# Two chained depthwise convolutions on TensorE: operand produced in two pieces, a shorter normalisation, the middle product kept in the output tile

## The chip, the cores and the metric

The kernel runs on one core of one Trainium2 chip. The metric is device time of one execution in microseconds (us). TensorE (PE) multiplies matrices and has a separate weight-load path (PEld), VectorE (DVE) and ScalarE (ACT) work elementwise, GpSimd (POOL) makes differences of columns, and SyncE (SP) issues nearly all DMAs.

## The reference

Everything is fp32. `x` is (32, 192, 56, 56). Twice, `x` is group-normalised (32 groups of 6 channels) and convolved channel by channel, and the result is added to `x`: first with a 31x31 filter and a bias, then with an 11x11 filter that is built from four points.

```python
def _gn(v, G=32, eps=1e-05):
    B_, C_, H_, W_ = v.shape
    g = v.reshape(B_, G, C_ // G, H_, W_)
    m = jnp.mean(g, axis=(2, 3, 4), keepdims=True)
    s = jnp.var(g, axis=(2, 3, 4), keepdims=True)
    return ((g - m) / jnp.sqrt(s + eps)).reshape(v.shape)

x = x + _L0_conv_ref(_gn(x), L0_conv_weight, L0_conv_bias_term)
x = x + _L1_conv_ref(_gn(x), L1_conv_weight_coord, L1_conv_radius, L1_conv_weights)
```

## The kernel before, in words

**Tiling.** The 128 partitions hold 4 bands of 16 image rows times 32 images. A job is one channel of one convolution, so there are 384 jobs: 192 FIRST jobs (31x31) and 192 SECOND jobs (11x11). They alternate in the list `PATTERN`: 12 slots, slots 0, 2, ..., 10 FIRST and 1, 3, ..., 11 SECOND. One turn of the loop over groups runs the 12 slots; iterations 0, 1 and the last ones are written out, 2 to 30 are a loop on DVE and ACT (2 to 29 on SP, 2 to 31 on PE and POOL). The second convolution of a group lags its first by some slots, since it needs the first one's sums for its own normalisation.

**One job on the engines.** ACT normalises a channel of `raw` into `images` (`normalise`, L763). DVE transposes it by 32x32 blocks into `xt` (`transpose_in`, L985). POOL makes differences of even and odd columns (`differences`: for FIRST L736, 960 columns, then L737, 512 columns, the differences of halves; for SECOND L739, 960 columns). ACT rounds the operand to its high part `x_hi` (`high`, L774 and L776) and DVE subtracts to get the low part `x_lo` (`low`, L1004 and L1006). PE then multiplies by banded (Toeplitz) matrices `toep` that DMAs fill from DRAM (L535), in three matmuls for each matrix: hi by hi, hi by lo, lo by hi (L1226). A FIRST job has 36 matmuls of 192 or 224 columns on the last 768 columns of its operand (the inner products: one of halves, two that share bank 3), then 48 of 352 to 448 columns on the first 960 columns (the outer products). A SECOND job has 9 inner matmuls (the middle product, bank 0) and 18 outer ones. At the end, ACT copies the middle product from PSUM to `p2` (`copy_p2`, L785 for FIRST, L788 for SECOND), DVE adds it to the halves (`combine`, L1013, FIRST alone) and to the outer products (`outputs`, L1023), transposes back into `yt` (`transpose_out`, L1032) and adds that to `raw` (`add_residual`, L1041).

**The order.** Each engine's order is written out by hand; semaphores tie them. While PE works on job n+1, DVE finishes job n and prepares job n+2 (`AHEAD` = 2). PE starts a job when `lo_ready` says that all of its `x_lo` is there, and when the outputs of the job two before have left PSUM. `T_RING` = 2: a channel's matrices are loaded over those of the channel two before, after that job's `conv_done`. SP goes through the same 12 slots: for each job it waits for `conv_done`, issues 8 DMAs of matrices, at slot 7 the four loads of a later group's `x`, at slots 5 and 11 the four stores of three channels.

**The normalisation.** `statistics` (L976) leaves 6 numbers for each half band of a channel (7 half bands, 6 channels). `normalisation` turns these into scale and bias in a chain of small DVE instructions, each waiting for the one before through `norm_chain` (`settle`). Two slots of a loop turn have it: slot 2 (for the second convolution of the group before) and slot 8 (for the first convolution of the next group). There it is split: `normalisation_begins` (aggregations L920 and L921, copies L926) stands ahead of `transpose_in`, `normalisation_ends` (L935 to L965) behind it, ahead of `combine`. ACT takes the root between (L792).

## Time and profile before

| | us |
|---|---|
| median of 3 runs (3794.69 to 3796.62) | 3796.46 |
| the profiled execution's own time | 3793.75 |
| its span | 3792.0 |
| PE busy | 3529.6 (93%) |
| DVE busy | 3284.3 (87%) |
| ACT busy, POOL busy | 1203.3, 1130.2 |
| granted TensorE clock, mean | 0.969 of full speed |
| DMA | 587.51 MB, mean 155 GB/s |

A busy share is time in which the engine had an instruction running. A window of the profile gives the same shares for a stretch, with the granted clock (1.00 is full speed) and the mean busy share of the 16 DMA engines, which goes to about 1.2 where they are full.

### The profile page before, as it was taken

What the parts mean: (1) busy time and instruction counts of PE and PEld (TensorE: products, weight loads), DVE (VectorE), ACT (ScalarE), POOL (GpSimd) and SP (SyncE); (2) the same over time, 40 slices, a digit from 0 to 9 for tenths busy, and PEclk for the clock granted to TensorE, in tenths of its full rate; (3) what the DMA queues carried; (4) which work ended last, traced back from release to release, by engine and by line L of the source; (5) the groups of instructions that cost most, each with busy time, mean ns of one, the idle gap of its engine ahead of it and who ended that gap; (6) DMA issues with size and microseconds to landing.
All of it is one profiled execution on the core that took longest, in us unless ns stands there. A gap on an engine that the chain in (4) does not pass through costs nothing.

```text
span 3792.0 us, 65954 instructions
## 1 busy us (share of the span) xinstructions
PE 3529.6 (93%) x21312; PEld 3349.7 (88%) x21312; DVE 3284.3 (87%) x4851; ACT 1203.3 (32%) x1442; POOL 1130.2 (30%) x660
## 2 busy tenths in 40 slices
PE   5889999999999999999999999999999999999997
PEld 5889898898898898988988988989889889899896
DVE  7888898888988888988889888889888898888887
ACT  3333333333333333333333333333333333333332
POOL 6113332223332233332223323333223323233332
PEclk9999999999999999999999999999999999999999
DMA  9987887879877878878788778888787887788673
GB/s 183 199 174 152 156 159 148 155 156 170 155 145 148 167 153 156 161 147 155 158 165 156 145 147 165 156 156 158 149 156 157 163 158 145 147 166 168 121 141 82
DMA packets 896128, 587.51 MB, mean 155 GB/s; under 512 B 501656, under 2 KB 858136, under 8 KB 895576
## 3 DMA queue, kind: packets, MB, share of 16 engines
q1 hardware_dynamic: 895416, 585.62, 80.2%
q14 instruction: 152, 1.25, 0.1%
q10 hardware_dynamic: 544, 0.38, 0.1%
q8 instruction: 16, 0.26, 0.0%
HBM read 499.20 MB, written 86.61 MB: 154 GB/s over the span
## 4 chain that ended last, share of the span: by engine, by line
PE 51%; DVE 28%; issue 15%; SPq 2%; POOL 1%; DMA 1%; DVEq 1%; ACT 0%; POOLq 0%; ACTq 0%
PE acc L1226 51%; DVE acc L1023 5%; DVE yt L1032 5%; DVE x_lo L1006 4%; DVE halves_tmp L939 3%; SPq L535 2%; DVE halves_tmp L941 2%; DVE part L976 1%; DVE raw L1041 1%; DVE p L1013 1%; DVE norm L965 1%; DMA toep<-padded 1%; DVE halves L926 1%; DVE x_lo L1004 0%; DVE agg L921 0%
## 5 line engine op out<-in xcount | busy, mean ns | idle before, releaser
L1226 PE MATMUL acc<-x_hi,toep 128*112 128x224 f32 (+5 forms) x14208 | 3406.6, 330 | 255.3 <-DVE x_lo L1006 178.0
L1226 PEld LDWEIGHTS acc<-x_hi,toep 128*112 128x112 f32 x14208 | 2454.5, 188 | 383.9 <-issue 182.3
L1226 PE MATMUL acc<-x_lo,toep 128*112 128x224 f32 (+5 forms) x7104 | 2343.7, 330 | 0.0
L1226 PEld LDWEIGHTS acc<-x_lo,toep 128*112 128x112 f32 x7104 | 1333.5, 188 | 51.0
L739 POOL TENSOR_TENSOR xt<-xt 128x960 f32<-128x960 f32 x188 | 423.6, 2253 | 1535.1 <-DVE xt L985 1535.1
L776 ACT ACTIVATE x_hi<-xt 128x256 fp32r<-128x256 f32 (+1 forms) x384 | 347.5, 905 | 1212.7 <-POOL xt L739 1193.9
L1023 DVE TENSOR_TENSOR acc<-acc,p 128x896 f32<-128x896 f32 x384 | 418.6, 1090 | 342.2 <-PE acc L1226 340.1
L736 POOL TENSOR_TENSOR xt<-xt 128x960 f32<-128x960 f32 x180 | 406.9, 2261 | 1016.8 <-DVE xt L985 1016.8
L774 ACT ACTIVATE x_hi<-xt 128x1472 fp32r<-128x1472 f32 x192 | 275.5, 1435 | 770.4 <-POOL xt L737 682.1
L985 DVE STREAM_TRANSPOSE xt<-images 128x960 f32<-128x960 f32 x384 | 451.1, 1175 | 14.0 <-ACT images L763 1.3
L1041 DVE TENSOR_TENSOR raw<-yt,raw 128x896 f32 (+1 forms) x384 | 422.4, 1100 | 30.3 <-DVE yt L1032 12.9
L763 ACT ACTIVATE images<-raw,norm 128x896 f32 (+1 forms) x384 | 439.3, 1144 | 16.8 <-DVE norm L965 16.8
L976 DVE BATCH_NORM_STATS2 part<-raw 96x6 f32 (+3 forms) x768 | 443.0, 609 | 0.0
L1032 DVE STREAM_TRANSPOSE yt<-acc 128x896 f32<-128x896 f32 x384 | 424.6, 1106 | 9.5
L1006 DVE TENSOR_TENSOR x_lo<-xt,x_hi 128x256 fp32r<-128x256 f32 (+1 forms) x384 | 396.7, 1033 | 3.1 <-ACT x_hi L776 3.1
L1004 DVE TENSOR_TENSOR x_lo<-xt,x_hi 128x1472 fp32r<-128x1472 f32 x192 | 317.3, 1653 | 3.6 <-ACT x_hi L776 3.6
L737 POOL TENSOR_TENSOR xt<-xt 128x512 f32<-128x512 f32 x180 | 231.8, 1288 | 0.0
L792 ACT ACTIVATE small<-small 32x1 f32<-32x1 f32 x64 | 12.9, 202 | 469.6 <-DVE small L947 469.6
L1013 DVE TENSOR_TENSOR p<-acc,p 128x448 f32<-128x448 f32 x192 | 116.8, 608 | 36.4 <-ACT p L785 29.1
L788 ACT ACTIVATE p<-acc 128x448 f32<-128x448 f32 x192 | 102.7, 535 | 100.6 <-DVE acc L1023 62.5
L939 DVE TENSOR_SCALAR halves_tmp<-halves,small 32x7 f32<-32x7 f32 x64 | 125.9, 1968 | 2.2
L785 ACT ACTIVATE p<-acc,bias_all 128x224 f32<-128x224 f32 x192 | 81.4, 424 | 0.0
(62 smaller groups left out, 456.2 us busy)
## 6 DMA issues: line engine op xcount, KB each, us to landing
toep<-padded SPq DMA_DIRECT2D x384, 322.0 KB
toep<-padded SPq DMA_DIRECT2D x384, 273.0 KB
toep<-padded SPq DMA_DIRECT2D x384, 217.0 KB
out_dram<-raw SPq DMA_DIRECT2D x189, 336.0 KB, 5.6
raw<-in_x_dram SPq DMA_DIRECT2D x93, 672.0 KB, 11.7
toep<-padded SPq DMA_DIRECT2D x768, 58.5 KB
toep<-padded SPq DMA_DIRECT2D x384, 80.5 KB
toep<-padded SPq DMA_DIRECT2D x384, 47.2 KB
```

The costliest lines, as they stand in the source:

```text
L736: nc.gpsimd.tensor_tensor(differences_held(), shifted_even(), repeated_odd(), ALU.subtract)
L739: nc.gpsimd.tensor_tensor(differences_held(), repeated_odd(), shifted_even(), ALU.subtract).then_inc(xd_ready, 1)
L763: nc.scalar.activation(image(ring(i, s, I_RING))[:, :, 1:1 + W], raw_rows(g, c), ACT.Identity, bias=norm[:, 0:1], scale=norm[:, 1:2]).then ...
L776: nc.scalar.activation(high_part, source, ACT.Copy).then_inc(hi_ready, 1)
L976: nc.vector.bn_stats(parts[0:held, k, c, :], raw_channel(g, c)[0:held, k * HALF:(k + 1) * HALF]).then_inc(parts_ready, 1)
L985: nc.vector.transpose(transposed(), blocks(image(ring(i, s, I_RING)))[:, :, ::-1, :]).then_inc(xt_ready, 1)
L1004: nc.vector.tensor_tensor(low_part, source, high_part.bitcast(F32), ALU.subtract)
L1006: nc.vector.tensor_tensor(low_part, source, high_part.bitcast(F32), ALU.subtract).then_inc(lo_ready, 1)
L1023: nc.vector.tensor_tensor(outer(i, s), outer(i, s), p2[:].unsqueeze(1).to_broadcast([P, 2, JH * B]), ALU.add).then_inc(y_ready, 1)
L1032: nc.vector.transpose(yt[:].rearrange("p (i s b) -> p s i b", s=2, b=B), outer(i, s).rearrange("p s (i b) -> p s i b", b=B)).then_inc(imag ...
L1041: nc.vector.tensor_tensor(rows, yt[:].rearrange("p (j h e) -> p h j e", h=HB, e=2), rows, ALU.add).then_inc(residual_added, 1)
L1226: last = nc.tensor.matmul(dst, toeplitz(toep, f, place_of_toep, part, w), src[:, cols], start=(m == matrices[0][0] and part == 0 and src i ...
```

## The change

**Operand in two pieces.** The 768 inner columns of a FIRST operand (480 of a SECOND one) are made, rounded and subtracted first, and the 960 outer ones after them, each with semaphores of its own. PE starts a job at `lo_inner_ready` and waits for `lo_ready` ahead of its outer products. On POOL and in the early iterations on DVE the differences of halves now come first, then a new copy of the 256 member columns to a contiguous place, then the 960-column difference.

**Normalisation in 15 steps.** The two aggregations, four copies and a hand-made mean and variance over 7 halves are replaced by four copies that gather all 6-number entries of an image (up to 72 columns of 32 partitions each) into `yt`, one `bn_aggr` over the 252 numbers, and one `tensor_scalar`; this stands whole ahead of `transpose_in`. The rest, from the reciprocal on, stands in slots 2 and 8 now behind `transpose_out` and the new `low_inner`.

**Middle product in the output tile.** `p2` is now `yt[:, 0:448]`, so ACT's copy of it waits for `residual_added` of the job before in place of `y_ready` of it.

```diff
-NORM_STEPS = 22
+NORM_STEPS = 15
@@ tiles
-        p2 = sb("p2", [P, JH * B])
         yt = sb("yt", [P, N])
+        p2 = yt[:, 0:JH * B]
+        gathered = yt[0:B, JH * B:JH * B + HALVES * CG * 6]
@@ operands
+        def inner_operand(i, s, tile):
+            if PATTERN[s][0] == FIRST:
+                start, size, at = AT_D2, N_HALVED * B, place(i, s) + 2 * N_D
+            else:
+                start, size, at = AT_EVEN + 1, N_D, place(i, s)
+            return xt[:, start * B:start * B + size], tile[:, at:at + size]
+        def outer_operand(i, s, tile):
+            at = place(i, s) + (0 if PATTERN[s][0] == FIRST else N_D)
+            return xt[:, AT_D * B:AT_D * B + 2 * N_D], tile[:, at:at + 2 * N_D]
@@ gpsimd, differences (FIRST)
-                    nc.gpsimd.tensor_tensor(differences_held(), shifted_even(), repeated_odd(), ALU.subtract)
-                    nc.gpsimd.tensor_tensor(*differences_of_halves(), ALU.subtract).then_inc(xd_ready, 1)
+                    nc.gpsimd.tensor_tensor(*differences_of_halves(), ALU.subtract)
+                    nc.gpsimd.tensor_copy(*members()).then_inc(xd_inner_ready, 1)
+                    nc.gpsimd.tensor_tensor(differences_held(), shifted_even(), repeated_odd(), ALU.subtract
+                                            ).then_inc(xd_ready, 1)
@@ scalar, high
-                act.wait_ge(xd_ready, n + 1)
+                if PATTERN[s][0] == FIRST:
+                    act.wait_ge(xd_inner_ready, first_ordinal(i, s) + 1)
+                else:
+                    act.wait_ge(xt_ready, n + 1)
...
+                source, high_part = inner_operand(i, s, x_hi)
+                nc.scalar.activation(high_part, source, ACT.Copy).then_inc(hi_inner_ready, 1)
+                act.wait_ge(xd_ready, n + 1)
+                source, high_part = outer_operand(i, s, x_hi)
                 nc.scalar.activation(high_part, source, ACT.Copy).then_inc(hi_ready, 1)
@@ scalar, copy_p2
-                    act.wait_ge(y_ready, n)
+                    act.wait_ge(residual_added, n)
@@ vector, normalisation_begins
-                link(nc.vector.bn_aggr(agg[:, 0, :], parts[:, 0].rearrange("p c k -> p (c k)")))
-                link(nc.vector.bn_aggr(agg[0:B * (BANDS - 1), 1, :],
-                                       parts[0:B * (BANDS - 1), 1].rearrange("p c k -> p (c k)")))
-                settle()
+                if positive(added):
+                    dve.wait_ge(residual_added, added)
                 for q in range(BANDS):
                     held = min(2, HALVES - 2 * q)
-                    link(nc.vector.tensor_copy(halves[:, :, 2 * q:2 * q + held].rearrange("b s k -> b k s"),
-                                               agg[B * q:B * q + B, 0:held, :]))
+                    link(nc.vector.tensor_copy(gathered[:, q * 2 * CG * 6:(q * 2 + held) * CG * 6],
+                                               parts[B * q:B * q + B, 0:held].rearrange("p k c n -> p (k c n)")))
...
+                link(nc.vector.bn_aggr(small[:, 2:4], gathered))
+                dve.wait_ge(norm_chain, f * NORM_STEPS + done[0])
+                nc.vector.tensor_scalar(small[:, 4:5], small[:, 3:4], EPS, None, ALU.add).then_inc(var_ready, 1)
@@ vector, normalisation_ends: the seven instructions ahead of the reciprocal
-                link(nc.vector.tensor_reduce(small[:, 0:1], halves[:, 0, :], AX_X, ALU.add))
...
-                link(nc.vector.tensor_scalar(halves_tmp[:, 0, :], halves[:, 0, :], small[:, 6:7], None, ALU.subtract))
-                settle()
-                link(nc.vector.tensor_tensor(halves_tmp[:, 1, :], halves_tmp[:, 0, :], halves_tmp[:, 0, :], ALU.mult))
...
@@ vector, the FIRST slots of the loop
-                        if early1:
-                            normalisation_ends(i * 2 + 1, norm1, job(i, LAST_FIRST) + 1)
                         combine(i, s)
...
                         outputs(i, s)
                         transpose_out(i, s)
+                        if after and not low_first:
+                            low_inner(*after)
+                        if early2:
+                            normalisation_ends(norm2_ordinal(group2), norm2, normalised)
+                        if early1:
+                            normalisation_ends(i * 2 + 1, norm1, job(i, LAST_FIRST) + 1)
                         if after and not low_first:
                             low(*after)
                         add_residual(i, s)
@@ tensor
-                    if k == before_outer and positive(n + 1 - P_RING):
-                        pe.wait_ge(image_ready, n + 1 - P_RING)
+                    if k == before_outer:
+                        pe.wait_ge(lo_ready, n + 1)
+                        if positive(n + 1 - P_RING):
+                            pe.wait_ge(image_ready, n + 1 - P_RING)
...
-                    pe.wait_ge(lo_ready, n + 1)
+                    pe.wait_ge(lo_inner_ready, n + 1)
```

On DVE at slot 8 of the loop, from the end of slot 7 to the transpose of the operand of slot 10 (L9xx are lines of each kernel; `parts1_ready` counts the statistics), before:

```order
L1006 TENSOR_TENSOR x_lo<-xt,x_hi 128x1440 [waits hi_ready]
L918 ISA
L919 MEMSET small 32x1 [waits parts1_ready]
L920 BN_AGGR agg<-part 128x2
L921 BN_AGGR agg<-part 96x2
L916 ISA
L926 COPY halves<-agg 32x2x2 [waits norm_chain]
L926 COPY halves<-agg 32x2x2 x2
L926 COPY halves<-agg 32x2
L982 REGISTER_ALU
L985 STREAM_TRANSPOSE xt<-images 128x15x2x32 [waits lo_ready,xn_ready]
```

The same place now:

```order
L1014 TENSOR_TENSOR x_lo<-xt,x_hi 128x960 [waits hi_ready]
L933 ISA
L934 MEMSET small 32x1 [waits parts1_ready]
L939 COPY yt<-part 32x72 [waits residual_added]
L939 COPY yt<-part 32x72 x2
L939 COPY yt<-part 32x36
L941 ISA
L942 MEMSET small 32x1 [waits norm_chain]
L943 BN_AGGR small<-yt 32x2
L944 REGISTER_ALU
L945 TENSOR_SCALAR small<-small 32x1 [waits norm_chain]
L986 REGISTER_ALU
```

The aggregation and the variance now both stand ahead of the transpose.

On DVE at the same slot, the stretch behind that transpose, from the last step of the normalisation to the residual, before:

```order
L965 COPY norm<-small 32x2 x3
L932 REGISTER_ALU
L1012 REGISTER_ALU [waits p2_copied,norm_chain]
L1013 TENSOR_TENSOR p<-acc,p 128x2x7x32 [waits u_done]
L1023 TENSOR_TENSOR acc<-acc,p 128x2x448 [waits conv_done,comb_ready]
L1032 STREAM_TRANSPOSE yt<-acc 128x2x14x32 [waits residual_added,y_ready]
L1004 TENSOR_TENSOR x_lo<-xt,x_hi 128x1472 [waits hi_ready]
L1006 TENSOR_TENSOR x_lo<-xt,x_hi 128x256
L1041 ISA [waits image_ready]
```

Now (the four steps between the reciprocal and the first copy left out):

```order
L989 STREAM_TRANSPOSE xt<-images 128x15x2x32 [waits lo_ready,xn_ready]
L1020 REGISTER_ALU [waits p2_copied]
L1021 TENSOR_TENSOR yt<-acc,yt 128x2x7x32 [waits u_done]
L1031 TENSOR_TENSOR acc<-acc,yt 128x2x448 [waits conv_done,comb_ready]
L1040 STREAM_TRANSPOSE yt<-acc 128x2x14x32 [waits residual_added,y_ready]
L1008 TENSOR_TENSOR x_lo<-xt,x_hi 128x768 [waits hi_inner_ready]
L952 REGISTER_ALU
L953 RECIPROCAL small<-small 32x1 [waits std_ready]
...
L969 COPY norm<-small 32x2 x3
L950 REGISTER_ALU
L1014 TENSOR_TENSOR x_lo<-xt,x_hi 128x960 [waits hi_ready,norm_chain]
L1049 ISA [waits image_ready]
```

The outputs, the transpose back and the inner `x_lo` now stand ahead of the reciprocal, where the whole rest of the normalisation stood ahead of them.

## Rows read from the trace of the kernel before

**Rows 1.** The page, busy time, share of the span and instructions of each engine.

```profile
PE 3529.6 (93%) x21312; PEld 3349.7 (88%) x21312; DVE 3284.3 (87%) x4851; ACT 1203.3 (32%) x1442; POOL 1130.2 (30%) x660
```

**Rows 2.** Waits of PE, whole span: line, what ended it, us, times, longest.

```profile
PE acc L1226 <- DVE x_lo L1006: 178.0, 61, 6.8
```

**Rows 3.** Timeline of DVE, four `outputs`: start us, us, instruction [idle before <-releaser].

```profile
1011.07 1.10 DVE L1023 TENSOR_TENSOR acc<-acc,p 128x896 f32<-128x896 f32 x1 [1.67 <-PE acc L1226]
...
1051.16 1.10 DVE L1023 TENSOR_TENSOR acc<-acc,p 128x896 f32<-128x896 f32 x1 [4.68 <-PE acc L1226]
...
1068.95 1.10 DVE L1023 TENSOR_TENSOR acc<-acc,p 128x896 f32<-128x896 f32 x1 [1.83 <-PE acc L1226]
...
1127.01 1.10 DVE L1023 TENSOR_TENSOR acc<-acc,p 128x896 f32<-128x896 f32 x1 [1.67 <-PE acc L1226]
```

**Rows 4.** Timeline of DVE at slot 8.

```profile
1023.13 0.32 DVE L920 BATCH_NORM_AGGREGATE agg<-part 128x2 f32<-128x36 f32 x1
...
1023.65 0.73 DVE L926 COPY halves<-agg 32x4 f32<-32x4 f32 x4
1024.42 1.18 DVE L985 STREAM_TRANSPOSE xt<-images 128x960 f32<-128x960 f32 x1
...
1025.84 2.12 DVE L939 TENSOR_SCALAR halves_tmp<-halves,small 32x7 f32<-32x7 f32 x1
1027.99 1.20 DVE L941 TENSOR_TENSOR halves_tmp<-halves_tmp 32x7 f32<-32x7 f32 x1
...
1030.01 0.15 DVE L949 RECIPROCAL small<-small 32x1 f32<-32x1 f32 x1 [0.27 <-ACT small L792]
...
1031.10 0.73 DVE L965 COPY norm<-small 32x2 f32<-32x2 f32 x4
...
1032.62 1.10 DVE L1023 TENSOR_TENSOR acc<-acc,p 128x896 f32<-128x896 f32 x1
```

**Rows 5.** Timeline of POOL in the same slot.

```profile
1025.68 2.26 POOL L736 TENSOR_TENSOR xt<-xt 128x960 f32<-128x960 f32 x1 [6.02 <-DVE xt L985]
1027.89 1.28 POOL L737 TENSOR_TENSOR xt<-xt 128x512 f32<-128x512 f32 x1
```

**Rows 6.** Line L939: count, duration ns min/median/max, first and last start.

```profile
L939 DVE TENSOR_SCALAR halves_tmp<-halves,small x64: 218/2114/2122, 26.4 to 3720.9; 32x7 f32<-32x7 f32 x64
```

**Rows 7.** Timeline of PE: slot 10's first matmul; slot 0's second matmul and its first outer `x_lo`.

```profile
1036.83 0.53 PE L1226 MATMUL acc<-x_hi,toep 128*112 128x224 f32 x1 [2.77 <-DVE x_lo L1006]
...
1056.31 0.27 PE L1226 MATMUL acc<-x_lo,toep 128*112 128x224 f32 x1
...
1060.18 0.36 PE L1226 MATMUL acc<-x_lo,toep 128*112 128x448 f32 x1
```

**Rows 8.** Window of PE: from, to, us, PE busy, granted clock, DMA share, GB/s.

```profile
1036.90:1040.00 3.10, 3.10 (x17) 0.50 1.22 204
```

**Rows 9.** Groups by form, 1000 to 3000 us: shapes, count | busy us, mean ns.

```profile
L1004 DVE TENSOR_TENSOR x_lo<-xt,x_hi 128x1472 fp32r<-128x1472 f32 x103 | 169.9, 1650 | 0.0
L774 ACT ACTIVATE x_hi<-xt 128x1472 fp32r<-128x1472 f32 x103 | 147.8, 1435 | 391.7 <-POOL xt L737 391.7
...
L1006 DVE TENSOR_TENSOR x_lo<-xt,x_hi 128x256 fp32r<-128x256 f32 x103 | 42.6, 414 | 0.0
...
L921 DVE BATCH_NORM_AGGREGATE agg<-part 96x2 f32<-96x36 f32 x35 | 8.9, 254 | 0.0
```

**Rows 10.** Timeline of the DMA issues on SP.

```profile
1041.08 6.32 SPq L535 DMA_DIRECT2D toep<-padded  x8
...
1051.25 6.13 SPq L535 DMA_DIRECT2D toep<-padded  x8
...
1069.60 6.25 SPq L535 DMA_DIRECT2D toep<-padded  x8
```

**Rows 11.** Windows: from, to, us, busy PE, PEld, DVE, ACT, POOL, clock, DMA share, GB/s.

```profile
1078.00:1087.00 9.00, 9.00 (x51) 8.60 (x50) 8.50 (x15) 2.44 (x3) 3.30 (x2) 1.00 1.18 211
...
1088.00:1089.00 1.00, 1.00 (x7) 0.90 (x5) 0.80 (x6) 1.00 (x1) 0.00 (x0) 1.00 0.69 100
```

More of the change, by code:

```diff
@@ L66 @@
 AT_D2 = AT_D + 2 * JE
-AT_ODD = AT_D2 + 2 * JZ + 1
+AT_MEMBERS = AT_D2 + 2 * JZ
+AT_ODD = AT_MEMBERS + JZ + 1
 N_T = AT_ODD + JE + 1
@@ L967, in normalisation_ends, with normalisation @@
                 assert done[0] == NORM_STEPS
-            def normalisation(f, g, parts, parts_ready, norm, normalised=None):
-                normalisation_begins(f, g, parts, parts_ready)
+            def normalisation(f, g, parts, parts_ready, norm, added, normalised=None):
+                normalisation_begins(f, g, parts, parts_ready, added)
                 normalisation_ends(f, norm, normalised)
@@ L1106, in _ @@
                 differences(0, s)
+                low_inner(0, s)
                 low(0, s)
@@ L1149, in iteration @@
                             statistics(part1, parts1_ready, i + 1, c1)
[L1150 to L1153 removed]
+                        if not early1 and s == NORM1_SLOT and measure_next:
+                            normalisation(i * 2 + 1, i + 1, part1, parts1_ready, norm1, n, job(i, LAST_FIRST) + 1)
                         combine(i, s)
@@ L1180, in iteration @@
                         if low_first:
+                            low_inner(*after)
                             low(*after)
@@ L1183, in iteration @@
                         if after and not low_first:
+                            low_inner(*after)
                             low(*after)
@@ L1189, in iteration @@
                             statistics(part1, parts1_ready, 1, c1)
-                        normalisation(1, 1, part1, parts1_ready, norm1, job(0, LAST_FIRST) + 1)
+                        normalisation(1, 1, part1, parts1_ready, norm1, n + 1, job(0, LAST_FIRST) + 1)
             iteration(0)
```

79 lines of the change are left out of this document (31 added, 48 removed).

## The prediction, made before the changed kernel ran

> **What bounds the kernel now.** First the busy shares [rows 1]: PE 3529.6 us of 3792.0, DVE 3284.3. PE leads, so the question is what its idle time waits for. In the waits of PE [rows 2] the last piece of `x_lo` is by far the largest: 178.0 us in 61 waits, 2.92 each. Next I looked where they fall. Two slots of a loop turn have them, slot 4 and slot 10, each the FIRST job that is prepared while DVE goes through a normalisation (slots 2 and 8). That is 2 x 29 in the loop and one in iteration 31: 59.
>
> What one of them costs in all is read from `outputs` on DVE, where it waits for PE and so marks the end of a job [rows 3]. The ends of slots 10 and 0 lie 17.79 us apart (1051.16, 1068.95), with no stall between: that is a pair of jobs at PE's own pace, and six are 106.74. From slot 6 to slot 6 of the next group it is 115.94 (1011.07, 1127.01). The difference is 9.20 a group, 4.60 for each stall. The idle part is 2.92; the rest, 1.7, is the clock: behind the stall before slot 10 [rows 7] the granted clock is 0.50 of full speed, 1.2 GHz in place of 2.4, for some 3 us [rows 8].
>
> Why `x_lo` is late stands in DVE's timeline at slot 8 [rows 4]. PE was ready for slot 10 at 1036.83 - 2.77 = 1034.06 [rows 7]; DVE did `outputs` of slot 8 at 1032.62 although that job had ended at 1011.07 + 17.79 = 1028.86. Before it stood the normalisation, and in that two instructions on 7 columns that took 2.12 and 1.20 us, L939 and L941. They end with POOL's two differences (1027.94 and 1029.17) [rows 5], and the shortest of the 64 L939, which ran in an early iteration, where POOL does no differences, took 0.218 [rows 6]. So DVE stands behind POOL there. The Trainium skill states this rule (SBUF — State Buffer, Who interferes with whom): a DVE instruction in a two-port mode, or with two SBUF inputs, and a GpSimd instruction that reads SBUF exclude each other for a whole instruction. The rule also bears on the new order, which I come back to in the rivals.
>
> **The change, part by part, at slot 8.** All times are on the trace's axis.
>
> *Beginning of the normalisation.* It begins at 1023.13, and 0.1 later now: a SECOND `x_lo` in two instructions pays the fixed part twice. From L1004 and L1006 [rows 9] a column costs (1650 - 414)/(1472 - 256) = 1.02 ns and the fixed part is 0.15 us. The four old copies of 4 columns took 0.73 [rows 4]; with 72 columns each, at 1.02 ns, about 1.0 (bounds 0.73, and 1.3 for twice the rate). The trace has no `bn_aggr` over 252 numbers; over 36 it took 0.254 [rows 9]. Below that it can't be; in proportion it would be 1.78; with only the extra 216 at 1.02 ns it is 0.47. I take 0.5, since all other rows of DVE follow a fixed part and a rate. With a memset, the `tensor_scalar` and the gaps, 0.35: 1.95 in place of 1.29. The transpose starts at 1025.2 (at the upper bounds 1026.8) and ends at 1026.3 (1027.9). What is late here costs nothing yet, because:
>
> *Combine and outputs.* Between the end of L965 and `outputs` stands `combine`, 0.8 with its gaps (1031.83 to 1032.62) [rows 4], so DVE stands before `outputs` at 1027.1 and waits for PE until 1028.86: 1.8 us of cover. `outputs` to 1030.0, `transpose_out` (1.12) to 1031.1.
>
> *Inner operand.* POOL after the transpose: halves 1.28, the new copy, then 2.26 [rows 5]. The copy of 256 columns with one input has no row; below it may cost nearly nothing, above 1.3, as much as 512 columns with two; I take 0.5, nearer to half of L737. Inner ready at 1026.4 + 1.28 + 0.5 = 1028.2; ACT on 768 columns takes less than the 1.435 of 1472 [rows 9], about 0.85: 1029.1. POOL is through at 1030.5, ACT with the outer part at 1031.5. Both stand ahead of DVE, so `low_inner` runs from 1031.1, 0.15 + 768 x 1.02 ns = 0.94, to 1032.1. PE wants it at 1034.06: 2.0 early. Here the stall goes.
>
> *Rest of the normalisation and outer operand.* From L949 to the end of L965 it took 1.8 [rows 4]; now 1032.1 to 1034.0, and the outer `x_lo` (960 columns, 1.13) to 1035.1. PE's inner products of a FIRST job take 3.87 at full clock (1056.31 to 1060.18, first `x_lo` matmul to first outer one) [rows 7], so the outer ones are due at 1037.9: 2.8 early. With every upper bound at once (copies, aggregation, POOL's copy) `low_inner` moves behind POOL's end at about 1032.9 and ends at 1033.8: still before 1034.06. The normalised channel that needs the result is ACT's next one but is transposed only after the residual, at about 1036.
>
> *What is late next.* In ordinary slots DVE waits for PE at `outputs` 1.67 to 4.68 us [rows 3], and the split of the SECOND operand adds 0.1 to a pair; that is covered. Removing the stall leaves DVE less time for slots 9 and 10. From `outputs` of slot 8 to standing before those of slot 10 it took 1051.16 - 4.68 - 1032.62 = 13.86 [rows 3, 4]; the last 1.8 of the normalisation now fall into that, and 0.1 for the split, 15.8: 1044.7, while PE ends slot 10 at 1028.86 + 17.79 = 1046.65. It is ahead by 1.9.
>
> *Middle product in `yt`.* ACT's copy now waits for the residual of the job before. On DVE a transpose (1.18) and a statistics instruction stand between that residual and the next `outputs` of a SECOND job; ACT needs 1.435 for 1472 columns [rows 9] and copies 448. Behind the copy on ACT's queue stand the rounding and the normalising of later jobs, whose inputs come from that same transpose. Cost nothing; in a FIRST slot the distance is larger.
>
> *SP and the loads.* A faster PE asks for loads sooner. Today SP issues a load in 6.1 to 6.3 us and reaches slot 10's with 3.85 us to spare (1047.40, 1051.25) [rows 10]. Then: the end of slot 10 at 1046.65, SP free at 1047.4, so the load starts at 1047.5, and the next one 18.35 later, as now (1051.25 to 1069.60: issue, stores, and 7.5 in which SP turns its loop): 1065.85. The load behind that, which slot 4 needs, ends today near 1089, where the DMA share falls from 1.18 to 0.69 [rows 11], 19.4 after 1069.60; then 1085.3. Slot 4 is due at 1046.65 + 2 x 17.79 + 5.2 = 1087.4 (5.2 is a SECOND job, 1034.06 - 1028.86). It is ready 2.1 early. This is the smallest margin that I find.
>
> **The sum.** 59 x 4.60 = 271.4 off. The longest wait, 6.8 [rows 2], is at the last normalisation, which stands whole in its slot; without the seven instructions I take 3 off. PE's added wait costs nothing: at that place the wait for `image_ready` stands already. 3793.75 - 271.4 - 3 = 3519.4 for an execution like the profiled one; the median of the runs lies 2.7 above it: **3522**.
>
> **The rivals.**
> - *The loads come late* (slot 4). For: the margin of 2.1 rests on DMAs whose pace I can't see beforehand, and SP has hardly any spare time left there. Against: they end as slack today. If late by 1 us: 1 + 1.7 of clock, once in 29 groups, 78 us: 3600. Chance 0.06.
> - *The normalisation slot is emptied only in part*: it needs 2 us more than my middle and more than all upper bounds together. Then a stall of 1 and the clock, 2.7 x 59 = 159: 3681. Chance 0.03.
> - *The order has no effect on what PE waits for*, say because ACT's part is late for a reason that I don't see: about 3790. Chance 0.02.
> - *DVE locked behind POOL in every slot: slower.* `low_inner` reads two SBUF tiles, and now stands ahead of the normalisation; if DVE doesn't wait for PE at `outputs`, it reaches it 3.0 after the transpose, while POOL's last difference runs until 4.1, and stands still up to 2.26, as L939 did. Once behind, it would never again wait for PE, so it would stay so. DVE's busy time is 3284.3/3792.0 x 115.94 = 100.4 a group; less 6 for the two locks that go, plus 12 x 2.26: 121.5, a bound above 115.94. 31 x 5.6 = 172 more than now: 3968. It decides where DVE lies behind PE at `outputs` in ordinary slots, which no row shows; the two normalisation slots are 1.8 ahead. Chance 0.04. The lock itself is the skill's rule that I named above; by it alone, without the wait at `outputs`, this would be the result.
>
> **How the numbers follow.** The forecast has 0.85. Its own range is 3505 to 3545: below, the first and last iterations, with stalls of their own, may give 15 more; above, a few stalls of some tenths. To hold 8 in 10 with what I may have missed in the loads, the range is 3503 to 3600. A change within 0.2% (7.6 us) can't be told from none: faster 0.94, same 0.02, slower 0.04.
>
> **What would show it.** After the change PE's waits for `x_lo` should be nearly gone in the loop, the granted clock near 1.00 in every slice but the first and last, `outputs` from slot 6 to slot 6 106.7 apart. The 7-column instructions are gone, no DVE instruction should last far over its length, and DVE should wait 1 to 2 us for PE at slots 2 and 8. It is wrong if PE waits for `toep` in the loop, if `low_inner` shows more than 0.94, or if the clock falls without a stall.

## The result and the profile after

| us | before | after |
|---|---|---|
| median | 3795.9 (3794.69 to 3796.62, 4 runs) | 3523.26 (3521.96 to 3524.39, 4 runs) |
| ratio | | 0.9282, 95% interval 0.9266 to 0.9298 |
| profiled execution, span | 3793.75, 3792.0 | 3523.32, 3521.5 |
| granted clock, mean | 0.969 | 0.994 |

3522 was predicted, with 3503 to 3600 as the range. The busy shares of the page, which answer to [rows 1]:

```profile
PE 3429.9 (97%) x21312; PEld 3266.5 (93%) x21312; DVE 3130.5 (89%) x4671; ACT 1297.9 (37%) x1634; POOL 1201.4 (34%) x840
```

PE does the same 21312 matmuls in 99.7 us less busy time, since its clock is no longer halved behind the stalls of the loop. DVE has 154 us less (the locks and the short instructions, less what the long aggregation and the split add); ACT and POOL have 95 and 71 more, for the split and the new copy, at 37% and 34% of the span.

The waits of PE over the whole span, as in [rows 2] (line, what ended it, us, times, longest):

```profile
PE acc L1244 <- DMA toep<-padded: 71.1, 10, 38.7
PE acc L1244 <- DVE x_lo L1008: 7.1, 2, 6.2
```

61 waits for `x_lo` have become 2; the waits for `toep` are of the start and the end, as before. In the window from 1000 to 3000 us (columns: from, to, us, busy PE, PEld, DVE, ACT, POOL, granted clock, DMA share, GB/s) PE is never idle and never slowed:

```profile
1000.00:3000.00 2000.00, 2000.00 (x12480) 1907.50 (x12479) 1798.64 (x2705) 747.66 (x937) 690.25 (x451) 1.00 0.88 169
```

The same window of the kernel before:

```profile
1000.00:3000.00 2000.00, 1902.26 (x11502) 1807.36 (x11501) 1750.62 (x2587) 634.75 (x758) 597.87 (x312) 0.97 0.81 156
```

The timeline of DVE over one turn of the loop, with the `outputs` of slot 0 (1004.57), slot 4 (1040.38), slot 8 (1075.68), slot 10 (1093.45) and the next slot 0 (1111.24) (start us, us, instruction, idle before). It answers to [rows 3, 4]:

```profile
1004.57 1.10 DVE L1031 TENSOR_TENSOR acc<-acc,yt 128x896 f32<-128x896 f32 x1 [1.76 <-PE acc L1244]
...
1040.38 1.10 DVE L1031 TENSOR_TENSOR acc<-acc,yt 128x896 f32<-128x896 f32 x1
...
1070.03 0.18 DVE L939 COPY yt<-part 32x72 f32<-32x72 f32 x1
...
1070.24 0.61 DVE L939 COPY yt<-part 32x72 f32<-32x72 f32 x3
...
1070.98 1.28 DVE L943 BATCH_NORM_AGGREGATE small<-yt 32x2 f32<-32x252 f32 x1
...
1072.46 1.18 DVE L989 STREAM_TRANSPOSE xt<-images 128x960 f32<-128x960 f32 x1
...
1075.68 1.10 DVE L1031 TENSOR_TENSOR acc<-acc,yt 128x896 f32<-128x896 f32 x1 [1.53 <-PE acc L1244]
...
1077.86 0.92 DVE L1008 TENSOR_TENSOR x_lo<-xt,x_hi 128x768 fp32r<-128x768 f32 x1
...
1079.06 0.15 DVE L958 TENSOR_TENSOR small<-small 32x1 f32<-32x1 f32 x1
...
1079.60 0.15 DVE L964 SCALAR_TENSOR_TENSOR small<-small 32x1 f32<-32x1 f32 x1
1079.78 0.73 DVE L969 COPY norm<-small 32x2 f32<-32x2 f32 x4
1080.55 1.16 DVE L1014 TENSOR_TENSOR x_lo<-xt,x_hi 128x960 fp32r<-128x960 f32 x1
...
1093.45 1.10 DVE L1031 TENSOR_TENSOR acc<-acc,yt 128x896 f32<-128x896 f32 x1 [1.97 <-PE acc L1244]
...
1111.24 1.10 DVE L1031 TENSOR_TENSOR acc<-acc,yt 128x896 f32<-128x896 f32 x1 [1.76 <-PE acc L1244]
```

From 1004.57 to 1111.24 a group takes 106.67, where it took 115.94. The instructions of the chain that took 2.12 and 1.20 are gone, and the short steps that are left, now behind `low_inner`, take 0.14 to 0.15 each. The row at 1075.68 is the one that makes this possible: DVE stands and waits for PE, and in that time and during `outputs` and `transpose_out`, which are not held, POOL does its three instructions. POOL in that slot, as [rows 5]:

```profile
1073.72 1.28 POOL L746 TENSOR_TENSOR xt<-xt 128x512 f32<-128x512 f32 x1 [7.24 <-DVE xt L989]
1074.95 0.40 POOL L747 COPY xt<-xt 128x256 f32<-128x256 f32 x1
1075.30 2.27 POOL L748 TENSOR_TENSOR xt<-xt 128x960 f32<-128x960 f32 x1
```

POOL is through at 1077.57 and `low_inner` begins at 1077.86. The first thing on DVE that reads two SBUF tiles behind the transpose comes after POOL, by 0.3 us. Its result is there at 1078.78, and PE takes up slot 10 at about 1080.7 (its second matmul is at 1080.83).

### The profile page after: what moved, and what is told of

Same layout as the page of the kernel before. It is cut to its first block, busy times and chain, and to the rows that moved or that the text cites. A ratio compares the mean times of both kernels' runs of the same rounds, so it can differ in the third digit from the quotient of the medians.

```text
span 3521.5 us, 66355 instructions
## 1 busy us (share of the span) xinstructions
PE 3429.9 (97%) x21312; PEld 3266.5 (93%) x21312; DVE 3130.5 (89%) x4671; ACT 1297.9 (37%) x1634; POOL 1201.4 (34%) x840
## 4 chain that ended last, share of the span: by engine, by line
PE 93%; DVE 2%; SPq 2%; DMA 1%; issue 1%; ACT 0%; POOL 0%; DVEq 0%; ACTq 0%; POOLq 0%
PE acc L1244 93%; SPq L545 2%; DMA toep<-padded 1%; DVE yt L1040 0%; DVE acc L1031 0%; DVE part L980 0%; DMA padded<-raw 0%; DVE xt L989 0%; SPq L555 0%; DVE x_lo L1014 0%; DVE x_lo L1008 0%; DVE raw L1086 0%; DVE acc L1071 0%; DVE xt L998 0%; POOL raw L709 0%
## 5 line engine op out<-in xcount | busy, mean ns | idle before, releaser
L1244 PE MATMUL acc<-x_hi,toep 128*112 128x224 f32 (+5 forms) x14208 | 3305.2, 323 | 84.6 <-DMA toep<-padded 71.1
L1031 DVE TENSOR_TENSOR acc<-acc,yt 128x896 f32<-128x896 f32 x384 | 418.6, 1090 | 266.1 <-PE acc L1244 265.0
L791 ACT ACTIVATE x_hi<-xt 128x960 fp32r<-128x960 f32 x384 | 386.9, 1008 | 572.5 <-POOL xt L751 323.7
L788 ACT ACTIVATE x_hi<-xt 128x768 fp32r<-128x768 f32 (+1 forms) x384 | 279.1, 727 | 837.3 <-POOL xt L747 651.7
L1014 DVE TENSOR_TENSOR x_lo<-xt,x_hi 128x960 fp32r<-128x960 f32 x384 | 442.4, 1152 | 2.2 <-ACT x_hi L791 0.2
L1008 DVE TENSOR_TENSOR x_lo<-xt,x_hi 128x768 fp32r<-128x768 f32 (+1 forms) x384 | 301.6, 785 | 0.0
L803 ACT ACTIVATE yt<-acc 128x448 f32<-128x448 f32 x192 | 104.9, 547 | 481.9 <-DVE raw L1049 469.0
L1021 DVE TENSOR_TENSOR yt<-acc,yt 128x448 f32<-128x448 f32 x192 | 114.4, 596 | 25.4 <-ACT yt L800 25.3
L800 ACT ACTIVATE yt<-acc,bias_all 128x224 f32<-128x224 f32 x192 | 85.9, 447 | 15.9 <-DVE raw L1049 2.0
L943 DVE BATCH_NORM_AGGREGATE small<-yt 32x2 f32<-32x252 f32 x64 | 81.9, 1280 | 0.9
```

Source lines behind the costliest of these rows:

```text
L791: nc.scalar.activation(high_part, source, ACT.Copy).then_inc(hi_ready, 1)
L1008: nc.vector.tensor_tensor(low_part, source, high_part.bitcast(F32), ALU.subtract).then_inc(lo_inner_ready, 1)
L1014: nc.vector.tensor_tensor(low_part, source, high_part.bitcast(F32), ALU.subtract).then_inc(lo_ready, 1)
L1031: nc.vector.tensor_tensor(outer(i, s), outer(i, s), p2.unsqueeze(1).to_broadcast([P, 2, JH * B]), ALU.add).then_inc(y_ready, 1)
L1244: last = nc.tensor.matmul(dst, toeplitz(toep, f, place_of_toep, part, w), src[:, cols], start=(m == matrices[0][0] and part == 0 and src i ...
```

## The experiments

The theory was that the *place* counts: what stands between a FIRST slot's transpose and its inner `x_lo`, together with POOL's lock on whatever short DVE instruction falls into POOL's three instructions. The rivals were that the shorter arithmetic removes the stall, or the split operand does. All times are of runs beside runs of the kernel before on the same chip (medians there 3794.7 to 3795.4).

| run | median us (range, runs) | ratio to before, 95% |
|---|---|---|
| ends_first | 3624.77 (3624.22 to 3625.5, 4) | 0.9549, 0.9533 to 0.9565 |
| whole_wait | 3594.57 (3593.79 to 3595.63, 4) | 0.9471, 0.9455 to 0.9487 |
| long_chain | 3522.63 (3521.39 to 3523.96, 4) | 0.9280, 0.9265 to 0.9296 |
| seven_ahead | 3762.77 (3762.56 to 3763.64, 4) | 0.9914, 0.9897 to 0.9930 |
| order_only | 3630.74 (3627.02 to 3632.13, 4) | 0.9568, 0.9552 to 0.9584 |
| split_only | 3705.2 (3703.51 to 3705.8, 4) | 0.9761, 0.9745 to 0.9778 |
| short_chain_only | 3739.99 (3738.99 to 3740.72, 4) | 0.9855, 0.9839 to 0.9871 |
| late_loads | 3673.51 (3667.08 to 3687.82, 5) | 0.9672, 0.9656 to 0.9688 |
| dve_behind | 3785.52 (3782.96 to 3786.54, 8) | 0.9974, 0.9963 to 0.9985 |
| dve_ahead | 3826.98 (3825.89 to 3827.65, 4) | 1.0082, 1.0066 to 1.0099 |
| residual_wait | 3795.87 (3792.5 to 3798.3, 10) | 1.0000, 0.9991 to 1.0010 |

### The changed kernel with one part undone

**ends_first**: the rest of the normalisation goes back to its old place, ahead of `combine`.

```diff
+                        if early2:
+                            normalisation_ends(norm2_ordinal(group2), norm2, normalised)
+                        if early1:
+                            normalisation_ends(i * 2 + 1, norm1, job(i, LAST_FIRST) + 1)
                         combine(i, s)
...
                             low_inner(*after)
-                        if early2:
-                            normalisation_ends(norm2_ordinal(group2), norm2, normalised)
-                        if early1:
-                            normalisation_ends(i * 2 + 1, norm1, job(i, LAST_FIRST) + 1)
```

> The changed kernel with one thing moved back: the end of the normalisation (from the reciprocal to the four copies into norm) stands again ahead of combine, right behind the transpose of the operand, where POOL then makes its differences. Theory 1 (a DVE instruction with two SBUF inputs stands still behind POOL): on the axis of the profile after, transpose ends at 1020.45, POOL works until about 1024.7, so the short multiplications wait for it as the 7-column instructions did before; the end of the normalisation at about 1025.8 in place of 1022.3, low_inner at 1029.5, PE due at 1027.5: a stall of 2.0 and 1.7 of slow clock at 59 places, about 3741 us, and instructions of 32x1 that last 0.5 to 2.3 us. Theory 2 (only the number of instructions ahead of low_inner counts): 1.85 us more ahead of outputs are covered by DVE's wait of 1.38 to within 0.5, low_inner at 1026.1, no stall: 3523 us.

The stalls are back, 59 more than in the changed kernel. Waits of PE:

```profile
PE acc L1244 <- DVE x_lo L1008: 94.3, 61, 6.2
```

The lock is back too, on instructions that have one column, and that take 0.15 in the changed kernel. DVE's timeline at a normalisation:

```profile
1046.45 1.13 DVE L958 TENSOR_TENSOR small<-small 32x1 f32<-32x1 f32 x1
1047.62 0.14 DVE L960 TENSOR_SCALAR small<-small 32x1 f32<-32x1 f32 x1
1047.80 0.15 DVE L962 TENSOR_TENSOR small<-small 32x1 f32<-32x1 f32 x1
1047.98 2.17 DVE L964 SCALAR_TENSOR_TENSOR small<-small 32x1 f32<-32x1 f32 x1
```

POOL at the same time:

```profile
1046.28 1.29 POOL L746 TENSOR_TENSOR xt<-xt 128x512 f32<-128x512 f32 x1 [7.28 <-DVE xt L989]
1047.52 0.39 POOL L747 COPY xt<-xt 128x256 f32<-128x256 f32 x1
1047.88 2.26 POOL L748 TENSOR_TENSOR xt<-xt 128x960 f32<-128x960 f32 x1
```

L958 ends (1047.58) where POOL's 512 columns end (1047.57), and L964 (1050.15) where its 960 end (1050.14). So the lock was never a matter of the two instructions that the change took out. It moved to the next ones with two inputs; what the shorter arithmetic removes is not the lock. The Trainium skill (SBUF — State Buffer, Who interferes with whom) states that a DVE instruction with two SBUF inputs contends with a GpSimd instruction that reads SBUF, and that one of them is blocked for the whole instruction of the other. The trace agrees, to 0.01 us and down to operands of one column.

The size was not as expected. A stall is (94.3 - 7.1)/59 = 1.48 of idle and costs (3623.3 - 3521.5)/59 = 1.73 in the span: hardly more than its own length. 2.0 of idle was expected, and 1.7 for the clock on top. Behind the 2.77 of the kernel before the clock fell [rows 7, 8]; behind a wait of 1.61 here it doesn't (window of PE: from, to, us, PE busy, granted clock, DMA share, GB/s):

```profile
1054.95:1058.00 3.05, 3.05 (x29) 1.00 1.21 205
```

**whole_wait**: PE waits for the whole `x_lo` at the start of a job; everything else stays.

```diff
-                    pe.wait_ge(lo_inner_ready, n + 1)
+                    pe.wait_ge(lo_ready, n + 1)
```

> The changed kernel, but PE waits at a job's start for the whole x_lo (lo_ready), as before. x_lo of slots 4 and 10 is whole at 1028.35 on the axis of the profile after, PE is due at 1027.5: a stall of 0.8 at 59 places. Theory 1 (a short stall costs its own length): 47 us, 3570. Theory 2 (each stall brings the half clock as well, 1.7 more): 147 us, 3670. Theory 3 (starting on the first piece is not needed): 3523.

```profile
PE acc L1244 <- DVE x_lo L1014: 61.8, 61, 7.2
```

(61.8 - 7.1)/59 = 0.93 of idle each, 1.20 in the span, 71 us in all. The clock stays at 1.00 here too; a window of PE (columns as above) behind a wait of 0.93:

```profile
1046.90:1050.00 3.10, 3.10 (x30) 1.00 1.22 205
```

So starting on the first piece is a real part of the change: in the changed kernel's slot 8, L1014 ends 1081.71, some three us behind L1008. PE waits 61 times in this run, as often as before the change, so the first piece is needed at the same 59 places, where the normalisation stands between the two.

**long_chain**: the old arithmetic in 22 steps comes back (two aggregations, small copies, mean and variance by hand), but all of it up to the variance stays ahead of the transpose.

```diff
-NORM_STEPS = 15
+NORM_STEPS = 22
...
-                link(nc.vector.bn_aggr(small[:, 2:4], gathered))
...
+                link(nc.vector.tensor_scalar(halves_tmp[:, 0, :], halves[:, 0, :], small[:, 6:7], None, ALU.subtract))
+                settle()
+                link(nc.vector.tensor_tensor(halves_tmp[:, 1, :], halves_tmp[:, 0, :], halves_tmp[:, 0, :], ALU.mult))
...
             def normalisation_ends(f, norm, normalised=None):
```

> The changed kernel with the old arithmetic of the normalisation (two bn_aggr, four copies of 4 columns, seven small instructions, 22 steps), all of it up to the variance ahead of the transpose, in the new order. Theory 1 (the place of the chain counts, not its length): the old beginning took 1.29 and the seven instructions, without POOL beside them, about 1.3, in all 2.6 against 2.43 of the new one: 3523 to 3526 us, no waits of PE for x_lo. Theory 2 (the shorter chain is what empties the slot): stalls come back at 59 places, 3650 or more.

3522.63 against 3523.26: the same. The number of steps is worth nothing in the new order. From the first instruction of the normalisation to the transpose it takes 2.62 (1070.94 to 1073.56), against 2.43 with one `bn_aggr`, and the wait at `outputs` behind it, in DVE's timeline, is shorter by about that:

```profile
1070.94 0.31 DVE L938 BATCH_NORM_AGGREGATE agg<-part 128x2 f32<-128x36 f32 x1
...
1073.56 1.18 DVE L1003 STREAM_TRANSPOSE xt<-images 128x960 f32<-128x960 f32 x1
...
1076.59 1.10 DVE L1045 TENSOR_TENSOR acc<-acc,yt 128x896 f32<-128x896 f32 x1 [1.35 <-PE acc L1258]
```

### The kernel before with one part alone

**seven_ahead**: only the seven instructions up to the variance go ahead of the transpose, where POOL does not run.

```diff
-            def normalisation_ends(f, norm, normalised=None):
...
                 link(nc.vector.tensor_scalar(halves_tmp[:, 0, :], halves[:, 0, :], small[:, 6:7], None, ALU.subtract))
...
+            def normalisation_ends(f, norm, normalised=None):
...
                 dve.wait_ge(std_ready, f + 1)
```

> The kernel before with one thing moved: the seven small instructions up to the variance stand ahead of the transpose, the rest of the normalisation stays behind it, ahead of combine. Theory 1 (DVE stands behind POOL with whatever two-input instruction comes there): the lock moves from the 7-column instructions to the multiplications of 32x1 behind the reciprocal; end of the normalisation at about 1031.9 against 1031.83: 3780 to 3800 us, no gain. Theory 2 (these two instructions are slow by themselves or stand behind POOL alone): 3.3 us are off the chain, x_lo is there at 1033.2, before PE at 1034.06: no stalls, 3525 us.

The groups of DVE from 1000 to 3000 us (shapes, count | busy us, mean ns | idle before):

```profile
L954 DVE TENSOR_TENSOR small<-small 32x1 f32<-32x1 f32 x35 | 74.0, 2115 | 1.2
...
L958 DVE TENSOR_TENSOR small<-small 32x1 f32<-32x1 f32 x35 | 36.2, 1035 | 1.2
...
L933 DVE TENSOR_SCALAR halves_tmp<-halves,small 32x7 f32<-32x7 f32 x35 | 7.6, 218 | 2.0
```

The one that stood 2.12 is at its own 0.22 (L933), and two later ones, one column wide, stand 2.12 and 1.04 in their place. The gain is 32 us of 272, twice what I had allowed, but it is the picture of the lock that moves: (159.2 - 7.1)/59 = 2.58 of idle is left at each stall, of 2.90.

**order_only**: besides, the rest of the normalisation goes behind `low`. The operand stays whole, the arithmetic is the old one.

```diff
-                        if early1:
-                            normalisation_ends(i * 2 + 1, norm1, job(i, LAST_FIRST) + 1)
...
                             low(*after)
+                        if early2:
+                            normalisation_ends(norm2_ordinal(group2), norm2, normalised)
+                        if early1:
+                            normalisation_ends(i * 2 + 1, norm1, job(i, LAST_FIRST) + 1)
                         add_residual(i, s)
```

> The kernel before with the order alone changed: the seven instructions up to the variance ahead of the transpose, the rest of the normalisation behind low, ahead of the residual. Operand in one piece, 22 steps, p2 in a tile of its own. On the axis of the profile before: transpose ends at 1026.8, POOL at 1030.5, ACT's x_hi is whole at 1032.3, x_lo at 1034.4, PE due at 1034.06. Theory 1 (the place of the normalisation against POOL is nearly all): a stall of 0.4 at 59 places without slow clock, about 3550 us, and no DVE instruction of 32 partitions over 0.25 us. Theory 2 (the two pieces are needed for most of the gain): 3650 or more.

It brings 165 of the 272, less than I expected (one stall of 0.4 at 59 places). No DVE instruction is locked; L954 and L958 take 0.15 again. But the stalls are spread, and two more FIRST slots of a turn have one. The waits of PE:

```profile
PE acc L1228 <- DVE x_lo L1006: 121.3, 120, 38.3
```

(38.3 of it is the start, which the other traces put down to `toep`.) That leaves about 0.7 each. How one of them arises, at slot 2, in the DVE timeline:

```profile
1051.58 1.69 DVE L1004 TENSOR_TENSOR x_lo<-xt,x_hi 128x1472 fp32r<-128x1472 f32 x1 [1.44 <-ACT x_hi L776]
```

DVE stands 1.44 for ACT, which rounds the whole operand after POOL has made all of it. The two more stalls, ahead of slots 0 and 6, have the same wait behind them (1.49 at 1015.04, 0.45 at 1070.46). With two pieces that wait is gone, because the first is ready while POOL still works at the second.

**split_only**: the changed kernel with the old normalisation in its old place. What stays of the change are the two pieces and the middle product in `yt`. Its edit is that of long_chain, with the seven instructions behind the transpose, and that of ends_first.

> The changed kernel with the old normalisation in its old place and arithmetic (seven instructions and the rest behind the transpose, ahead of combine, 22 steps); the operand in two pieces and p2 in yt stay. The locks stay, so outputs starts at about 1032.6 on the axis of the profile before, x_lo's inner piece is there at 1035.7, PE due at 1034.06. Theory 1 (the idle time shrinks from 2.9 to 1.65 and the clock doesn't fall behind so short a stall, as it did not behind 1.5 us in the run with the end first): 1.9 at 59 places in place of 4.6, about 3635 us. Theory 2 (the clock falls also here): 3735. Theory 3 (two pieces alone suffice): 3525.

The result lies between my two numbers: 2.00 of idle a stall, 3.09 in the span.

```profile
PE acc L1258 <- DVE x_lo L1022: 125.3, 61, 5.8
```

The DVE timeline shows the lock in its old place. POOL has three instructions there, and a third one of DVE, L959 between these two, takes 0.30:

```profile
1008.66 1.16 DVE L957 TENSOR_SCALAR halves_tmp<-halves,small 32x7 f32<-32x7 f32 x1
...
1010.17 2.19 DVE L961 TENSOR_TENSOR halves_tmp<-halves_tmp,halves 32x7 f32<-32x7 f32 x1
```

Behind stalls of this size the clock falls sometimes. Two windows of PE, behind a wait of 1.92 and behind one of 2.15:

```profile
1018.80:1021.90 3.10, 3.10 (x30) 1.00 1.23 193
...
1074.50:1077.60 3.10, 3.10 (x22) 0.71 1.22 203
```

**short_chain_only**: the kernel before with the gathering copies, the one `bn_aggr` over 252 numbers and the one `tensor_scalar`. These stand ahead of the transpose, so it is seven_ahead with the shorter arithmetic; the order is the old one otherwise.

```diff
-NORM_STEPS = 22
+NORM_STEPS = 15
+        gathered = yt[0:B, JH * B:JH * B + HALVES * CG * 6]
...
+                link(nc.vector.bn_aggr(small[:, 2:4], gathered))
...
             def normalisation_ends(f, norm, normalised=None):
-                link(nc.vector.tensor_reduce(small[:, 0:1], halves[:, 0, :], AX_X, ALU.add))
...
```

> The kernel before with the new normalisation of 15 steps alone (gather, one aggregation and the variance ahead of the transpose, the rest behind it, ahead of combine); one-piece operand. Theory 1: as with the seven instructions moved ahead (3763), since the multiplications still stand behind POOL: 3750 to 3770 us. Theory 2 (fewer steps are worth their instructions, and the lock goes with the 7-column ones): 3600 or less.

```profile
PE acc L1216 <- DVE x_lo L996: 146.6, 61, 7.1
```

55 us, 10 more than the best of what I expected: 2.36 of idle in each stall in place of 2.90, and the clock doesn't fall fully behind all of them any more. Two windows of PE, behind waits of 2.22 and 2.46:

```profile
1025.20:1028.30 3.10, 3.10 (x30) 1.00 1.23 201
...
1081.30:1084.40 3.10, 3.10 (x19) 0.58 1.21 213
```

Of the 55 us, seven_ahead has 32 without any shorter arithmetic. The other 23 (3762.77 to 3739.99) are the arithmetic's own: the idle time of a stall goes from 2.58 to 2.36, about the 0.19 by which 2.43 is shorter than 2.62. So in the old order it pays a little; behind the new order there is nothing left for it to pay on (long_chain).

### The margins

**late_loads**: the changed kernel, and at slot 1, ahead of the load that slot 4 needs, SP issues eight small copies inside DRAM (256 bytes each, not used by anything).

```diff
                         sp.wait_ge(conv_done, n)
+                        if s == 1:
+                            for k in range(8):
+                                sp.dma_start(aside[k:k + 1, :], padded1[0:1, 0, 0:64]).then_inc(aside_done, 16)
                         next_toeplitz(*earlier(i, s))
```

> The changed kernel, with 8 more DMAs of 256 bytes between two DRAM tensors issued by SP at slot 1 of each group ahead of the load of slot 0's matrices, about 0.35 to 0.7 us each on SP, 3 to 5.5 us in all. In the profile after, the matrices for slot 4 land 2.4 us (at least 1.3) before PE wants them. Theory 1 (that margin is real and the smallest): PE waits for toep at slot 4 of each group, 1 to 3 us in 29 or 30 groups, 3555 to 3620 us. Theory 2 (the loads have more slack than it seems, since they share the DMA engines): 3523.

The DMA issues on SP:

```profile
1047.49 5.01 SPq L626 DMA_DIRECT2D aside<-padded  x8
1052.73 35.36 SPq L547 DMA_DIRECT2D toep<-padded  x40
```

The waits of PE:

```profile
PE acc L1249 <- DMA toep<-padded: 177.4, 38, 39.1
```

And slot 4's first matmul in its timeline:

```profile
1066.07 0.53 PE L1249 MATMUL acc<-x_hi,toep 128*112 128x224 f32 x1 [3.02 <-DMA toep<-padded]
```

The load comes 5.24 later (1047.49 to 1052.73) and PE waits 3.02 at slot 4, so the slack of the changed kernel was about 2.2 us at this place; I had worked out 2.1. By the mean wait of the run, 3.8, it is 1.4. This also prices the first rival: (177.4 - 71.1)/28 = 3.8 of idle a group, and (3686.0 - 3521.5)/28 = 5.9 in the span, for the clock falls behind this stall. The runs of this kernel spread more than those of the others (3667.08 to 3687.82), and its median is above the 3555 to 3620 that I gave.

**dve_behind** and **dve_ahead**: the fourth rival says that the new order becomes the slower one when DVE no longer waits for PE at `outputs`. To get there, nine statistics instructions over 192 columns, whose result nothing reads, are added in each FIRST slot of the loop: behind the transpose and ahead of `combine`, or ahead of the transpose.

```diff
+            def more(count):
+                for k in range(count):
+                    last = nc.vector.bn_stats(aside[:, k, :], bias_all[:])
+                last.then_inc(aside_ready, 1)
...
+                    if not peeled and conv == FIRST:
+                        dve.wait_ge(aside_ready, (i - 2) * 6 + s // 2 + 1)
+                        more(9)
                     if after:
                         transpose_in(*after)
```

(This is dve_ahead; in dve_behind the same lines stand ahead of `combine`.)

> The changed kernel with 9 more bn_stats of 192 columns (about 0.27 us each, 2.4 in all; they read the bias, their result is not used) on DVE in each FIRST slot of the loop, behind the transpose of the operand, ahead of combine. DVE's waits for PE before outputs are 8.0 us a group now, 14.5 are added: DVE becomes the bound, and is behind PE at every outputs. It reaches low_inner 5.4 us after the transpose, POOL is through at 4.1: no lock. A group 106.7 + 6.5 = 113.2: about 3710 us, and L1008 stays at 0.92 us.

> The same 9 instructions in each FIRST slot, but ahead of the transpose of the operand. DVE is behind PE in the same way, and now reaches low_inner 3.0 us after the transpose, while POOL works until 4.1. Theory 1 (my rival of the prediction: low_inner then stands behind POOL's last difference): L1008 (768 columns) lasts about 2 us in place of 0.92 in the FIRST slots, 6 x 1.1 a group more than with the instructions behind the transpose: 119.8 a group, about 3910 us. Theory 2 (no lock for large instructions, or POOL stands behind instead): 3710 us like the other.

Both have the same instructions. Ahead of the transpose they cost 41 us more (3785.52 to 3826.98), and the kernel with all of the change in it is then slower than the one before (3826.98 against 3795). DVE's timeline of dve_ahead:

```profile
1044.62 2.05 DVE L1010 TENSOR_TENSOR x_lo<-xt,x_hi 128x768 fp32r<-128x768 f32 x1
```

POOL there:

```profile
1043.58 2.27 POOL L750 TENSOR_TENSOR xt<-xt 128x960 f32<-128x960 f32 x1
```

`outputs` no longer waits for PE (at 1042.45 it follows its neighbour at once), so the inner `x_lo` comes 1.2 us before POOL's end (1045.85) and stands. The groups from 1000 to 3000 us say how often; first dve_ahead:

```profile
L1010 DVE TENSOR_TENSOR x_lo<-xt,x_hi 128x768 fp32r<-128x768 f32 x102 | 150.3, 1473 | 0.0
```

then dve_behind, where the added instructions hold DVE back until POOL is through:

```profile
L1010 DVE TENSOR_TENSOR x_lo<-xt,x_hi 128x768 fp32r<-128x768 f32 x103 | 94.4, 917 | 0.0
```

So the mechanism of the rival exists, but smaller than I had written: 1.1 in place of 2.26 where it strikes, and only in half of the FIRST slots (in the others statistics already stand between, and in the SECOND slots the inner `x_lo` takes 0.65 in both runs). 3910 was expected and 3827 came. dve_behind itself came out at 116 us a group where I expected 113.2, and so at 3786 in place of 3710. DVE's waits in dve_behind, and then in dve_ahead, show an item that the other traces hide under the wait for PE:

```profile
DVE xt L991 <- issue: 83.0, 29, 3.8
...
DVE aside L1038 <- issue: 38.2, 28, 2.5
```

At the turn of its loop DVE does nothing and waits for nothing that the profile shows, for 83.0/29 = 2.9 us in dve_behind, about the 2.8 that my 113.2 lacked, and for 38.2/28 = 1.4 in dve_ahead. So the 41 us understate the lock: it adds 6 x 0.56 = 3.3 us a group (1473 against 917 ns), and the shorter idle time at the turn takes 1.5 of these back; the spans (3825.9 and 3781.8) differ by 1.5 a group. Why the turn costs less in one run than in the other stays open.

**residual_wait**: the kernel before, with the wait that the middle product's move to `yt` brings.

```diff
-                    act.wait_ge(y_ready, n)
+                    act.wait_ge(residual_added, n)
```

> The kernel before; ACT's copy of the middle product waits for residual_added of the job before in place of y_ready, as the change does since p2 lies in yt (here p2 keeps a tile of its own). Theory 1 (covered by a transpose and statistics on DVE): 3795 us within 0.2%. Theory 2 (the copy comes late at some outputs): 3800 to 3850, with waits of DVE L1023 for ACT.

1.0000 of the time before. The later wait costs nothing in the old order; under the new one, where PE goes faster, it was not taken out alone. What is known there is that PE is not idle between 1000 and 3000 us.

## Why the prediction was right, and where it was not

**The sum.** 59 stalls at 4.60 was right: (3792.0 - 3521.5)/59 = 4.58. The group, taken as 106.74, came out at 106.67. Reading the pace of two undisturbed jobs from `outputs`, and so the price of a stall with its clock, is what made this number.

**The last normalisation.** The 3 us that I took off for it did not come. PE's longest wait for `x_lo` went from 6.8 to 6.2. The median came out right all the same, because I had added 2.7 for the distance of the profiled execution to the median of the runs, and the changed kernel has no such distance (3523.32 against 3523.26). Two errors of one size stand against each other, and that the median fits to 1.3 us is in part luck.

**The beginning of the normalisation.** Predicted 1.95, measured 2.43 (1070.03 to 1072.46). (My terms 1.0, 0.5 and 0.35 add up to 1.85; the 0.1 for the split is in the 1.95 and again in the start.) The term that was mis-sized is `bn_aggr` over 252 numbers: 0.5 taken, 1.28 measured, with 1.78 as the upper bound. I had given it DVE's 1.02 ns for a number; from the 36 numbers in 0.254 [rows 9] to 252 in 1.28 it is 4.75 ns for each. The copies took 0.79 in place of 1.0. What hid the difference is the cover ahead of `outputs`: 1.8 predicted, 1.53 left. With little cover this mistake would have been a stall.

**The inner operand.** POOL's copy 0.40 (0.5 taken), the inner `x_lo` 0.92 (0.94), the outer 1.16 (1.13). The claim that POOL stands ahead of DVE held, but by 0.3 us (1077.57 to 1077.86), less than the 0.6 that the text had (1030.5, 1031.1). ends_first and dve_ahead show what lies on the other side of it. The inner `x_lo` is ready 1.9 ahead of PE (1078.78, about 1080.7), where 2.0 was predicted.

**What is late next.** At slot 10 DVE is 1.97 ahead (1.9 predicted). Slot 2's normalisation I had not worked through, only slot 8's. Behind it, at slot 4, four statistics stand ahead of `outputs`, where slot 10 has none, and there DVE has no wait at all (the row at 1040.38). PE had no wait for it either, so nothing was lost, but the smallest margin on DVE is there and not at the place that I looked at.

**The loads.** Predicted 2.1 early, measured 1.4 to 2.2 by late_loads. My price for that rival, 2.7 a group, was for 1 us of lateness; it was not put to the test at that size.

**The split's own weight.** The prediction treated the change as one. The runs part it: from the changed kernel, the place of the normalisation is worth 101 us (ends_first), the start on the first piece 71 (whole_wait), the arithmetic 0 (long_chain), the wait of the middle product 0 as far as it was tried (residual_wait). From the kernel before, the same parts alone bring 165 (the place), 90 (the two pieces and `yt`) and 55 (the arithmetic with its seven instructions moved ahead; 23 for the arithmetic itself). They don't add up, since all of them cut at the same stall. Two things went wrong in my expectations of these runs. The idle time was off: 2.0 expected and 1.48 measured in ends_first, 1.65 and 2.00 in split_only, 0.4 at 59 places and 0.7 at 119 in order_only. And I took the clock as all or nothing: 1.7 behind a stall, or none. From the spans and the waits:

| kernel | idle a stall | cost a stall | clock behind one |
|---|---|---|---|
| whole_wait | 0.93 | 1.20 | 1.00 |
| ends_first | 1.48 | 1.73 | 1.00 |
| split_only | 2.00 | 3.09 | 1.00 or 0.71 |
| short_chain_only | 2.36 | 3.66 | 1.00 or 0.58 |
| before | 2.90 | 4.58 | 0.50 |

The two short ones cost about 0.25 more than their idle time, with no lower clock in the windows, and the surcharge grows to 1.7 only with the long ones. Why the clock falls behind one wait of about 2 and not behind another stays open.

## What to carry to other kernels

A short instruction can stand for the length of another engine's long one. If its time in the trace differs from its shortest in the same trace, look at what ends with it, and move it to where that engine is idle, or behind a wait that has to be made anyway; taking the held instructions out of the chain hands the lock to the next ones (32 of 272 us here). Price a stall by the distance between two ends in an undisturbed stretch, not by its idle time, and take the price of a long stall for no short one. When an order relies on an engine that waits, say how much it waits: that number is the margin of the change.

## What the hardware showed that was not expected

- The lock between POOL and DVE holds for operands of one column: a `tensor_tensor` on 32x1 stood 1.13 and a `scalar_tensor_tensor` on 32x1 2.17 in ends_first, while the `tensor_scalar` between them, during POOL's copy, took 0.14. On 32x7 a `tensor_scalar` was held as well (1.16 in split_only). One on 32x1 was not: in short_chain_only it took 0.14 at 1018.00, while POOL's 512 columns ran from 1017.91 to 1019.20.
- Around the end of one of POOL's instructions, or during its short copy, DVE gets a short two-input one through (L962 at 1047.80 in ends_first, 0.15), and then stands for the whole of POOL's next. One that began during the copy (L959 at 1009.85 in split_only) took 0.30 and ended with it.
- `bn_aggr` over 252 numbers takes 1.28 us, about 4.75 ns a number over the 36-number form, against 1.02 ns a column for DVE's two-input arithmetic.
- The turn of DVE's loop costs it 2.9 us in dve_behind and 1.4 in dve_ahead, the two runs in which DVE sets the pace.
